# Reordering ScalarE's copies and dealing the dense passes anew in a fused graph-layer and product-key attention kernel

## The reference

```python
# layer 1: graph
n = layernorm(x)
deg = adj.sum(1);  msg = (adj^T @ (n @ W_msg)) / max(deg, 1)      # 0 where deg == 0
x = x + relu(n @ W_upd + msg + bias)
# layer 2: product-key attention, for each head h
n = layernorm(x);  q = (n @ Wq_h) * 128**-0.5
s0, i0 = top_k(sim_side0, 16);  s1, i1 = top_k(sim_side1, 16)    # 128 keys a side
w, pick = top_k(s0[:, None] + s1[None, :], 16);  w = softmax(w)
row = i0 + 128 * i1 at the picks
k = sum_16 w * keys_table_h[row];  v = sum_16 w * values_table_h[row]
out_h = softmax(causal(q @ k^T)) @ v
x = x + concat_h(out_h) @ Wo
```

## Time and profile before

| | |
|---|---|
| median of 3 runs | 9134.44 us (9129.34 to 9146.46) |
| profiled execution | 9143.0 us, span of its core 9141.0 us |
| mean granted TensorE clock | 0.973 |
| busy: PE, PEld, DVE, ACT, POOL | 91%, 73%, 83%, 63%, 72% |
| instructions | 197626 |
| DMA | 1752.90 MB, mean 192 GB/s |

### The profile page before, as it was taken

One profiled execution on the slowest core, in us unless ns is written; L12 is line 12 of the kernel. 1 busy time (PEld: TensorE's weight loads), 2 busy tenths in 40 slices (PEclk: granted clock), 3 DMA queues, 4 the chain that ended last, 5 costly groups with the idle time before them and its releaser, 6 DMA issues.

```text
span 9141.0 us, 197626 instructions
## 1 busy us (share of the span) xinstructions
PE 8357.0 (91%) x55616; PEld 6715.8 (73%) x55616; DVE 7594.9 (83%) x33772; ACT 5770.7 (63%) x16755; POOL 6550.2 (72%) x6923
## 2 busy tenths in 40 slices
PE   6999999999999999989999999999999999999999
PEld 5777777777777777777777777777777777777777
DVE  7888888888888888888888888888888888888886
ACT  4666666666666666656666566665666666666666
POOL 5777676776767767677676776767767677676776
PEclk8999999999999999999999999999999999999999
DMA  4655656555565565655556565565655656556565
GB/s 140 214 185 187 200 185 212 185 188 197 183 208 185 192 199 185 207 183 196 191 184 212 179 202 189 184 208 180 205 184 183 210 182 201 185 186 208 179 212 172
DMA packets 470655, 1752.90 MB, mean 192 GB/s; under 512 B 123760, under 2 KB 141552, under 8 KB 371056
## 3 DMA queue, kind: packets, MB, share of 16 engines
q0 software_dynamic: 331776, 906.41, 32.3%
q1 hardware_dynamic: 137712, 832.82, 26.0%
HBM read 1734.54 MB, written 4.19 MB: 190 GB/s over the span
## 4 chain that ended last, share of the span: by engine, by line
PE 50%; DVE 35%; issue 7%; ACT 5%; DMA 1%; POOL 1%; DVEq 1%; ACTq 0%; POOLq 0%
PE dense_ps L606 25%; DVE wide L1325 11%; PE wideT_ps L592 7%; PE comb_ps L752 5%; DVE hits L1284 3%; ACT expo L880 3%; DVE onehot L1185 2%; DVE chosen L1197 2%; DVE onehot L1192 2%; PE front_ps L554 2%; PE score_ps L648 2%; PE comb_ps L582 1%; PE score_ps L636 1%; DMA tab<-in_extra 1%; PE probT_ps L654 1%
## 5 line engine op out<-in xcount | busy, mean ns | idle before, releaser
L481 POOL DMA_INDIRECT got<-in_table,rows x6912 | 6547.5, 947 | 2576.1 <-issue 2122.2
L606 PE MATMUL dense_ps<-tab,wideT 128*128 128x256 f32 x20480 | 4989.1, 387 | 20.4 <-DMA tab<-in_extra 18.4
L606 PEld LDWEIGHTS dense_ps<-tab,wideT 128*128 128x128 f32 x20480 | 3776.4, 193 | 715.7 <-issue 228.9
L1325 DVE SCALAR_TENSOR_TENSOR wide<-const_ps,rank,expo 128x128 f32<-128x128 f32 x10240 | 2862.9, 344 | 953.7 <-PE wideT_ps L592 653.0
L880 ACT ACTIVATE expo<-sim_d,shift 128x128 f32<-128x128 f32 x8192 | 2597.9, 391 | 304.7 <-DVE wide L1325 301.5
L812 ACT ACTIVATE wideT<-wideT_ps 128x512 f32<-128x512 f32 x2560 | 1515.1, 592 | 1463.8 <-PE wideT_ps L592 1459.4
L592 PE MATMUL wideT_ps<-ident,wide 128*128 128x128 f32 x10240 | 1579.5, 278 | 306.1 <-ACT wideT L812 297.1
L592 PEld LDWEIGHTS wideT_ps<-ident,wide 128*128 128x128 f32 x10240 | 1242.7, 143 | 560.6 <-issue 346.1
L752 PE MATMUL comb_ps<-got,spread 128*32 128x256 f32 x13824 | 837.4, 383 | 9.4 <-DMA got<-in_table,rows 9.4
L880 ACT ACTIVATE expo<-sim_x,shift 128x128 f32<-128x128 f32 x2048 | 649.8, 392 | 78.0 <-DVE wide L1325 77.8
L752 PEld LDWEIGHTS comb_ps<-got,spread 128*32 128x32 f32 x13824 | 406.4, 110 | 346.6 <-issue 78.8
(11 more groups left out here) (179 smaller groups left out, 7285.4 us busy)
## 6 DMA issues: line engine op xcount, KB each, us to landing
tab<-in_dense SPq DMA_DIRECT2D x512, 1024.0 KB
tab<-in_extra SPq DMA_DIRECT2D x256, 1024.0 KB
got<-in_table,rows POOLq DMA_INDIRECT x6912, 2.8
adj_i<-in_adj SPq DMA_DIRECT2D x16, 1024.0 KB
x_in<-in_x SPq DMA_DIRECT2D x16, 256.0 KB, 6.9
out<-fin SPq DMA_DIRECT2D x16, 256.0 KB
tab<-in_wqpk_t SPq DMA_DIRECT2D x1, 512.0 KB, 10.6
tab<-in_keys_t SPq DMA_DIRECT2D x1, 512.0 KB, 14.9
```

Source lines behind the costliest of these rows:

```text
L481: pool.indirect_dma_start(out=got[got_no(n)][:, g, :], out_offset=None, in_=table, in_offset=bass.IndirectOffsetOnAxis(ap=rows[:, t * GATH ...
L606: mm = pe.matmul(dense_ps[:, v * 2 * D:(v + 1) * 2 * D], wideT[k % 2][:, q * P:(q + 1) * P], tab[c % 2][:, key % KEYS, :], start=(begins a ...
L1325: last = dve.scalar_tensor_tensor(wide[k % 2][:, q, :], count_ps[:, v, :], rank1[:, COLUMNS[j][v], key:key + 1], expo[k % 2][:, q, :], ALU ...
```

## The change

Four things change, in batches 0 to 14 all of them, in batch 15 all but the table and the graph messages.

1. ScalarE does one pass of `w[0]` less ahead of the kv copy, and that pass right behind it. In slots with one pass there the copy comes first. TensorE and VectorE keep their order.
2. The passes of `MIDDLE` are dealt anew; their sum stays 160. Slots 1, 3, 5, 8, 20, 21 and 22 have one more, 9 and 25 two more; slots 2, 4, 6, 11, 18, 19 and 27 one fewer, 10 and 26 two fewer.
3. `best_dense` part 0 moves from the start of the third preparing slot (2, 8, 22) to the end of the second (1, 7, 21), behind `lay` and ahead of `add`.
4. VectorE takes the first half of the graph messages in slot 13, between `w[3]` and `hot_rows`, and the second half with the rest of the layer in slot 14 as before.

```diff
 MIDDLE = [
-    SEVEN, FIVE, SIX, FOUR,
-    SEVEN, SIX, SIX, FIVE,
-    SIX, FIVE, SIX, SIX,
+    SEVEN, SIX, FIVE, FIVE,
+    SIX, SEVEN, FIVE, FIVE,
+    SEVEN, SEVEN, FOUR, FIVE,
     SIX, FIVE, FIVE, FIVE,
-    SEVEN, SIX, SEVEN, SEVEN,
-    SIX, FIVE, FIVE, FOUR,
-    SIX, FOUR, SEVEN, SIX]
+    SEVEN, SIX, SIX, SIX,
+    SEVEN, SIX, SIX, FOUR,
+    SIX, SIX, FIVE, FIVE]
...
# ScalarE, batch
-                k = passes(b, k, w[0], first, last)
+                k = passes(b, k, max(w[0] - 1, 0), first, last)
                 if n != EXTRA_SLOT:
                     act.wait_ge(combined, b * TILES + gathers(n) + 1)
                     copy(kv[:, t, :], comb_ps[:, 0:2 * D]).then_inc(kv_copied, 1)
+                k = passes(b, k, min(w[0], 1), first, last)
...
# VectorE
-        def gnn_msg(b, first_batch=False):
-            for i in range(2):
+        def gnn_msg(b, halves=(0, 1), first_batch=False):
+            for i in halves:
...
+            if 1 not in halves:
+                return
...
-                if o == 2:
-                    best_dense(group_d, 0)
                 k = passes(b, k, w[1], last)
...
                 if n == 14 and not last:
-                    gnn_msg(b + 1)
+                    gnn_msg(b + 1, (1,))
...
                 k = passes(b, k, w[3], last)
+                if n == 13 and not last:
+                    gnn_msg(b + 1, (0,))
                 hit_part(3)
...
                     lay(nt)
+                if o == 1:
+                    best_dense(group_d, 0)
                 if o == 0:
                     rank_dense(of_d, group_d, 2)
```

## The result

The changed kernel takes 9022.69 us (9021.24 to 9027.13), the kernel before beside it 9136.51: ratio 0.9875, 95% interval 0.9858 to 0.9893, 114 us less. The forecast was 9090: the right way, inside the range, but 45 us of the 114. In batches 2 to 13 a batch takes 8.1 us less, where the sum said 3.0.

A forecast was written before the change was run, and what follows sets the result against it. The prediction took the order, not one engine, as the limit: TensorE and VectorE hand the end back and forth. Slot terms summed to -3.6 us a batch, -3.0 after the clock, -45 in 15 batches: 9090, range 8990 to 9155.

The forecast's parts named there:

- the sum: Gains and losses by groups of slots, followed through one batch: -3.6 us, or -3.0 after 0.6 for the lower clock.
- the clock: Slots 2, 10 and 14: a new stall expected in slot 10 with lower clock, delaying slot 11; 0.6 us a batch lost.
- the short kv waits: TensorE's waits for the kv copy, as in slot 5: 0.39 us each, gone once the copy comes over a pass earlier.
- edit 3: Moving best_dense part 0, 1.1 us of VectorE in slots 7 and 21, half in slot 1: 0 to -1.1 each.
- So 1.6 of the 3.22 goes and the rest becomes a wait for VectorE: Slot 2: of TensorE's 3.22 us kv copy wait 1.6 goes; the rest becomes waiting for VectorE's first pass.
- the row of slots 1 and 2: Slots 1 and 2: VectorE's tail 2.9 us later, then VectorE, one pass lighter, ends slot 2 0.9 ahead; -0.9 a batch.
- +4.4 predicted for slots 21 and 22: Slots 21 and 22: two passes more, only partly taken up by TensorE's 6.05 us idle behind VectorE; +4.4 us a batch.
- slots 9 and 10 +2.8: Two passes more in slot 9 need 4.4 us, two fewer in slot 10 give back only 2.2; +2.8 a batch.
- Two signs of being wrong: Slot 2 shorter by more than 2 us; a new ScalarE wait for the combine with TensorE's transposes behind it.
- The kv waits taken off whole: Rival: about two thirds of TensorE's 216.6 us of kv copy waits come off, -145 us, 8990; chance 0.2.
- The rival by the rule of the Trainium skill: VectorE is the engine to relieve and loses no work, so the time stays 9134; nothing gained has chance 0.14.
- The slow rival: Slots 9 and 10: TensorE stands in slot 10, clock falls, slot 11 starts late; +2.8 a batch, 9176; chance 0.2.

The follow-up runs named there:

- filling the stalls: Kernel before plus 110 unused unit-matrix transposes a batch where TensorE stands in slots 2, 14, 22, 25 and 26: 9051.35 us, ratio 0.9908.
- filling the stall: Changed kernel plus unused unit-matrix transposes ahead of the first w[3] pass of slots 8, 10, 14, 22 and 26: 8981.88 us, ratio 0.9828.

## Why the prediction was right in its direction and wrong in its size

The sum missed 5.1 us a batch. No single term carries that. Three failed: the clock, which was counted against the change and was for it; the short kv waits, which gave more than their own length; and edit 3, which was left at about 0.

**The clock, the step that failed in its mechanism.** The prediction saw the 0.84 of slot 2 and the transposes of 1.06, and took them for a side effect: "I take off 0.6", against the change. It priced the waits and not what TensorE did behind them. In the kernel before, the lower clock lasted 26.5 us a batch (mean over batches 2 to 13); in the changed one 14.2. In slots 2 and 26 the copy alone gave 1.85 and 1.15 us a batch, and filling the stalls 1.81 and 1.14. So the sentence "So 1.6 of the 3.22 goes and the rest becomes a wait for VectorE" was right as a timeline (1.51 left) and missed what it did to the slot. How much of the 8.1 us is the clock's can only be estimated: filling the stalls gave 5.9 us for 19.1 us less of lower clock, 0.31 each, and at that price the 12.3 us less of the changed kernel are 3.8. It is a rough price, for it is near 0 in slots 10 and 25, and the kernel with edits 1 and 3 gains 8.2 us a batch with 19.6 us of lower clock left. And the row of slots 1 and 2 doesn't show it: slot 2 became 3.6 shorter and slot 1 3.2 longer, together 0.4 where 0.9 was forecast.

**Edit 1's short waits, undersized.** The 0.39 of slot 5 was measured as -0.59 for that slot. With the copy alone slots 0, 5, 7, 16, 18 and 27, which TensorE paces in part, gave 0.6 to 1.2 each, 4.4 together. The prediction gave 0.4 each to a few of them. Against that stand 2.0 lost again in slots 8, 9, 14 and 22; in 8 the lower clock had risen from 0.9 to 4.8 us a batch. That a wait of 0.39 gives more than 0.39 was measured and not explained.

**Edit 3, mis-sized.** It was bounded by 0 and -1.1 for each place and then left at about 0 in the sums; it measured 40 us, 2.4 a batch in batches 2 to 13: 0 in slots 1 and 2, 0.8 in slots 7 and 8, 1.3 in slots 21 and 22, the rest spread. In slots 7 and 8 it gives 0.6 at equal clock, in slots 21 and 22 0.1: there it pays by the clock.

**The largest single miss** in the table, +4.4 predicted for slots 21 and 22 and +2.7 measured, is the clock too. The prediction worked from batch 8, in which the kernel before had the clock up in slot 22. There, and in the other three such batches, the change costs 3.9. By the mean the kernel before lost 1.3 us to the lower clock in slot 22 (the filled stall gave them back), and the changed kernel has none of it there.

**Edit 4** was taken as 0 and is 0 within what the runs tell (3 us): slot 13 grew by 1.2 and slot 14 shrank by 1.1, the 1.11 of the earlier trace rows moved from one to the other along a VectorE that doesn't pause.

**Edit 2.** The forecast was good here: slots 9 and 10 +2.8 (+2.7, though its own prices, 4.4 less 2.2, give 2.2; the slots measured +4.3 and -1.6), slots 18 to 20 -3.9 (-4.0), slots 27 and 0 -3.1 (-3.5). What the prediction never did was add up the dealing by itself. Alone it is worth nothing (ratio 1.0003), on top of the others it costs about 13 us.

**The signs that it named.** The waits for the kv copy went and those for the blocks rose, slots 9 and 10 took 40.46 (40.4 named), slots 18 and 19 took 3.6 less (about 5 named), slots 21 and 22 took 3.9 more in batch 8 (about 5), but by the mean 2.7. Two signs of being wrong came as well: slot 2 was shorter by 3.6, more than the 2 named, by its pass fewer and the copy (the table alone made it 1.9 shorter, the copy alone 1.85); and ScalarE waits for the combine, though the waits show nobody held up by it. Slot 14 shorter by over 1 was named as a sign that VectorE pauses ahead of it; it was shorter by 1.1, with slot 13 longer by 1.2, so the sign was badly chosen: it should have been the two together.

**The rivals.** The kv waits taken off whole would have been 8990; the copy alone gave 85 of those 145 us, and in the two longest waits no more than filled stalls gave. The rival by the rule of the Trainium skill (Perfetto Trace Analysis, Identifying the Most-Contended Engine), that nothing is gained while VectorE keeps its work, fell: VectorE is as busy (7591.3) and the time is 1.25% less. The slow rival named the right place, slots 9 and 10, and the size of 2.8, but not the reason: the clock did fall in slot 10 (2.3 us a batch at the lower level), yet filling the stall changed slots 10 and 11 by 0.1 only, so VectorE covered it. Slots 25 and 26, where it had a loss too, were together 0.9 shorter.

**What stays open.** How much of the 98 us that TensorE was busy less counts in the time: the filled stalls tell it for slots 2, 14, 22 and 26, where it counts, and for 10 and 25, where it doesn't. It was not found why slot 8 gets the lower clock in some kernels and not in others with the same passes in it, and in one kernel in some batches and not in others.

## What to carry to other kernels

Price a stall of TensorE with what it does to the instructions behind it: read the granted clock of each slot, in more than one batch, and the duration of the same instruction behind a long and a short wait. Then ask whether another engine covers it: VectorE did so in slots 10 and 25. A wait that only changes its place can still pay if it is cut into shorter ones. And when a table of many numbers is changed together with an order, run the table alone: here it took back about a tenth of what the order gave.

## What the runs showed of the hardware

Work that nobody needs made the kernel faster. In the kernel before, 110 unused transposes of 0.12 us a batch, in stalls of 2.4 to 4.9 us, brought the mean granted clock from 0.973 to 0.989 and the time from 9137.76 to 9051.35; 15 of them a batch, in the same places, left it at 0.974 and the time at 9130.45. With the clock at its lower level of 1.2 GHz four transposes took 1.06 to 1.09 us, at 2.4 GHz 0.60 to 0.66. The Trainium skill says so in TensorE: Matmul & The Clock Gate, What's actually happening: "the default state is throttled, and activity releases the throttle." The trace agrees, with slot 14 at 0.84 with 3 transposes and 1.00 with 34. What I had not expected is the price: in batch 8 the slot took 20.76 us with 3 of them and 18.02 with 34, and by the mean of batches 2 to 13 2.2 us more, so that a wait of under 5 us had cost about 2 us more behind it.
